# Rotary products of a second attention: from GpSimd and VectorE to VectorE alone

## The reference, cut to what matters

```python
# end of the mixture of experts: each token sums its four experts' rows
routed = sum over the 4 chosen slots of  weight * expert_ffn(x)
h = h + routed + shared
# second attention, 16 query heads, 4 key heads, head size 32
Q = layernorm(h) @ Wq ; K = layernorm(h) @ Wk ; V = layernorm(h) @ Wv
Q = Q * cos + rotate_half(Q) * sin
K = K * cos + rotate_half(K) * sin
A = softmax(causal(Q K^T / sqrt(32))) ; h = h + (A V) @ Wo
```

## Time and profile before

| | before |
|---|---|
| median of 3 runs | 1511.07 us (1508.02 to 1511.49) |
| the profiled execution's own time | 1511.43 us |
| its span, first to last instruction | 1509.5 us |
| PE busy | 1294.1 us (86%) |
| DVE busy | 896.4 us (59%) |
| ACT busy | 629.5 us (42%) |
| POOL busy | 308.6 us (20%) |
| mean granted TensorE clock | 0.922 of full |

### The profile page before, as it was taken

One profiled execution on the slowest core, in us unless ns is written; L12 is line 12 of the kernel. 1 busy time (PEld: TensorE's weight loads), 2 busy tenths in 40 slices (PEclk: granted clock), 3 DMA queues, 4 the chain that ended last, 5 costly groups with the idle time before them and its releaser, 6 DMA issues.

```text
span 1509.5 us, 30358 instructions
## 1 busy us (share of the span) xinstructions
PE 1294.1 (86%) x10660; PEld 829.6 (55%) x10674; DVE 896.4 (59%) x1865; ACT 629.5 (42%) x1066; POOL 308.6 (20%) x336
## 2 busy tenths in 40 slices
PE   6878899999999999986759999999972868768997
PEld 3446677777777877764424444444531656424443
DVE  5776455555565555668653555544332665578886
ACT  3445344444444444442314444444431333236664
POOL 2443000000000000000012233333267853010000
PEclk9997999999999999996779999999995869789999
DMA  5111343524435352422315767865268520000000
GB/s 181 68 66 43 100 178 138 200 105 174 142 127 204 135 185 109 156 85 89 124 70 178 257 227 257 303 242 170 98 125 133 85 43 3 2 1 8 21 21 32
DMA packets 44238, 184.26 MB, mean 122 GB/s; under 512 B 8688, under 2 KB 9200, under 8 KB 36368
## 3 DMA queue, kind: packets, MB, share of 16 engines
q0 software_dynamic: 21280, 95.41, 20.3%
q1 hardware_dynamic: 19440, 75.41, 14.3%
q10 hardware_dynamic: 3456, 12.58, 2.3%
HBM read 135.65 MB, written 47.73 MB: 121 GB/s over the span
## 4 chain that ended last, share of the span: by engine, by line
PE 55%; DVE 18%; issue 13%; POOL 7%; ACT 4%; DMA 2%; DVEq 1%; ACTq 0%; POOLq 0%; SPq 0%
PE ps L929 14%; PE ps L931 13%; PE ps L930 13%; POOL h L506 3%; PE ps L1036 3%; PE ps L1019 3%; PE ps L1255 2%; DVE ff L1976 2%; DVE amf L1983 1%; PE ps L1120 1%; PE ps L1052 1%; POOL rt_out L466 1%; PE ps L1348 1%; PE ps L1366 1%; POOL qraw L539 1%
## 5 line engine op out<-in xcount | busy, mean ns | idle before, releaser
L929 PE MATMUL ps<-nT_hi,wa_hi 128*128 128x368 f16 x448 | 147.9, 330 | 11.8 <-DVE wa_lo L1395 8.1
L930 PE MATMUL ps<-nT_lo,wa_hi 128*128 128x368 f16 x448 | 147.3, 329 | 0.0
L931 PE MATMUL ps<-nT_hi,wa_lo 128*128 128x368 f16 x448 | 147.0, 328 | 0.1
L496 POOL DMA_INDIRECT xg<-xrow,idx x61 | 61.4, 1007 | 276.7 <-PE ps L1120 121.5
L1559 DVE TENSOR_TENSOR a<-sq,E 92x368 f32<-92x368 f32 x64 | 31.7, 534 | 136.3 <-ACT sq L694 136.3
L1731 DVE SCALAR_TENSOR_TENSOR nrm<-ps,xg,nrm 128x256 f32<-128x256 f32 x61 | 29.5, 484 | 133.3 <-ACT nrm L737 112.1
L930 PE MATMUL ps<-wa_lo,nT_hi 128*92 128x128 f16 (+1 forms) x560 | 107.1, 235 | 0.0
L929 PE MATMUL ps<-wa_hi,nT_hi 128*92 128x128 f16 (+1 forms) x560 | 107.1, 235 | 0.0
L931 PE MATMUL ps<-wa_hi,nT_lo 128*92 128x128 f16 (+1 forms) x560 | 107.1, 235 | 0.0
L929 PE MATMUL ps<-wide,xT 128*128 x244 | 93.6, 383 | 12.9 <-issue 8.2
L491 POOL DMA_DIRECT2D wsp<-we_sp x16 | 8.6, 539 | 446.6 <-DVE we_sp L1395 446.6
(11 more groups left out here) (302 smaller groups left out, 3326.1 us busy)
## 6 DMA issues: line engine op xcount, KB each, us to landing
we_st<-in_we POOLq DMA_DIRECT2D x16, 1536.0 KB, 6.8
wsp<-we_sp POOLq DMA_DIRECT2D x16, 1536.0 KB, 5.4
wide<-wsp SPq DMA_DIRECT2D x16, 1536.0 KB
yslot<-yt POOLq DMA_DIRECT2D x61, 256.0 KB
wq_st<-in_ffq SPq DMA_DIRECT2D x24, 512.0 KB, 6.0
wq_st<-in_ffq ACTq DMA_DIRECT2D x24, 512.0 KB
wide<-in_wa SPq DMA_DIRECT2D x10, 1024.0 KB, 4.8
xt<-in_x SPq DMA_DIRECT2D x12, 512.0 KB, 3.5
```

The lines of the kernel that those rows point to most:

```text
L496: pool.indirect_dma_start(Q["xg"][:, g % 4, :].bitcast(U32), None, xrow, bass.IndirectOffsetOnAxis(ap=idx[:, g:g + 1], axis=0)).then_inc(x ...
L929: nc.tensor.matmul(dst, lhs[0], rhs[0], start=start, stop=False)
L930: nc.tensor.matmul(dst, lhs[0], rhs[1], start=False, stop=False)
L931: return nc.tensor.matmul(dst, lhs[1], rhs[0], start=False, stop=stop)
```

## The change

POOL no longer computes rotary products: `cosine` is gone. In `rotate(c, j)` DVE does the shuffle, the cosine product and the sine product, for every chunk and piece. POOL's list in that stretch keeps gathers, roots and memsets in another order: `shares(2, 1)` now stands ahead of `turned_root(0)`, `shares(2, 2)` ahead of `turned_root(1)`, `shares(3, 0)` behind `shares(2, 3)`, and `turned_root(2)` still behind `shares(3, 2)`. `rotated(c)` gets one count of a spare semaphore (`passed`) behind its wait.

```diff
--- before.py
+++ after.py
@@ -534,41 +534,25 @@
                 x = slice(GT * g, GT * g + GT)
                 root(rc_ask, 2 + g, rt_in[:, x], rt_out[:, x], rc_done)
 
-            def cosine(c, j):
-                pool.wait_ge(f_sh, 5 * c + j + 1)
-                nc.gpsimd.tensor_tensor(Fm["qraw"][:, j, :], Fm["qraw"][:, j, :], cosT[:], ALU.mult).then_inc(f_cos, 1)
-                if c and j < 4:
-                    nc.gpsimd.tensor_tensor(Fm["qs"][:, j, :], Fm["qs"][:, j, :], sinT[:], ALU.mult).then_inc(f_cos, 1)
-
             for j in range(TOPK):
                 shares(0, j)
                 shares(1, j)
             pool.wait_ge(m_y, VT)
             shares(2, 0)
+            shares(2, 1)
             turned_root(0)
             nc.gpsimd.memset(Fm["qp"][:, :, :, SL:], 0.0).then_inc(f_pad, 1)
+            shares(2, 2)
+            turned_root(1)
+            shares(2, 3)
             shares(3, 0)
-            turned_root(1)
-            cosine(0, 0)
-            shares(2, 1)
-            cosine(0, 1)
-            cosine(0, 2)
-            shares(2, 2)
-            cosine(0, 3)
-            cosine(0, 4)
-            shares(2, 3)
             pool.wait_ge(wa_lo, UNITS + 1)
             nc.gpsimd.memset(st_a[:], 0.0).then_inc(f_pad, 1)
             shares(3, 1)
-            for j in range(5):
-                cosine(1, j)
             shares(3, 2)
             turned_root(2)
             shares(3, 3)
             turned_root(3)
-            for c in range(2, CH):
-                for j in range(5):
-                    cosine(c, j)
             pipeline(pool, NT, [(0, lambda k, p, half: root(rf_ask, k, rt_in[:, p:p + 1], rt_out[:, p:p + 1], rf_done))])
             for n, x in enumerate((slice(0, EARLY), slice(EARLY, NT))):
                 root(rq_ask, n, rq_in[:, x], rq_out[:, x], rq_done)
@@ -1829,14 +1813,15 @@
                 dve.sem_inc(passed, 1)
                 V.stream_shuffle(Fm["qs"][:, j, :], Fm["qraw"][:, j, :],
                                  [(x + HD // 2) % HD for x in range(HD)]).then_inc(f_sh, 1)
-                if c == 0 or j == 4:
-                    dve.wait_ge(f_sh, 5 * c + j + 1)
-                    dve.sem_inc(passed, 1)
-                    V.tensor_tensor(Fm["qs"][:, j, :], Fm["qs"][:, j, :], sinT[:], ALU.mult).then_inc(f_cos, 1)
+                dve.wait_ge(f_sh, 5 * c + j + 1)
+                dve.sem_inc(passed, 1)
+                V.tensor_tensor(Fm["qraw"][:, j, :], Fm["qraw"][:, j, :], cosT[:], ALU.mult).then_inc(f_cos, 1)
+                V.tensor_tensor(Fm["qs"][:, j, :], Fm["qs"][:, j, :], sinT[:], ALU.mult).then_inc(f_cos, 1)
 
             def rotated(c):
 
                 dve.wait_ge(f_cos, 10 * c + 10)
+                dve.sem_inc(passed, 1)
                 if c:
                     dve.wait_ge(f_sc, c)
                 else:
```

## The result

The changed kernel took 1515.76 us (median of 6, 1514.63 to 1516.86), the kernel before 1510.45 us (median of 6, 1508.02 to 1511.49): ratio 1.0037, 95% interval 1.0024 to 1.0050. It is slower, by 5.3 us between the medians and 0.37% by the ratio. The profiled execution took 1516.86 us, with a span of 1515.1 us, 5.6 us more than before.

What follows compares the result with a forecast made beforehand. The second attention's start was taken to hang on `turned_root(0)` in POOL's list, each chunk being one chain. 5.7 - 2.65 - 1.9 - 0.1 + 1.85 + 1.5 = +4.4 on 1511.43 gave 1515.8 us, range 1510.5 to 1520.

Steps and rivals of the forecast that it cites:

- The root: Second attention's start: three gathers at 1.85 us ahead of `turned_root(0)`, uncovered, delay the first norm; +5.7 us.
- The landing wait: First gather of `shares(2, 1)` waits for slot 0 of the same tile to land: 0 to 1 us, 0.15 taken.
- Price of a product: Rotations on DVE: products start 0.46 us apart, so one rotation occupies DVE for 1.63 us.
- The rival of no overlap: Each DVE product occupies its full 0.54 us; chunks 1 to 3 cost 2.2 us more, 1518.0 us; chance 0.03.
- Stretching by gathers: POOL's gathers lengthen DVE's products in chunks 0 and 1: +4.7 us, 1520.5 us; chance 0.09.
- Chunks 1 to 3: DVE's rotations and weights up to `kr` replace the wait for POOL: -0.1, +1.85 and +1.5 us.
- Chunk 0: Before the first scores: PE becomes the limit, so only 2.66 of the 5.3 us `kr` waited come back; -2.65 us.
- Clock: `scores(0)` on PE: with the pause before it gone, it should run like `scores(2)`, 5.10 for 7.00 us; -1.9 us.
- The zero for the other three: Other three runs of scores may each gain or lose 1 to 2 us; their sum was taken as zero.
- The forecast's side of the 0.3% bound: Whether the time exceeds 1515.6 us, 0.3% slower: slower 0.51, same 0.43, faster 0.06.

Runs made afterwards that it cites:

- second pair of profiles: Kernel before and changed kernel each profiled again, unchanged: one run each, 1509.48 us and 1513.46 us.
- a division: Changed kernel with the old POOL order; in chunks 1 to 3 POOL does both products of pieces 0 to 2, DVE the others: 1500.57 us, ratio 0.9933.
- two versions with a short and a long pause: Changed kernel with chunk 0's `qp` addition repeated, two extra additions or three, to delay the first scores: 1518.40 us and 1523.87 us.

## Why the prediction was right, and where its terms were not

*The root.* Right in mechanism and place, +5.7 forecast, +6.1 in both pairs of profiles. The landing wait was 0.6 us and not 0.15. Putting the gathers back took 6.8 us off.

*Price of a product.* Right: pairs 0.46 apart, all 40 between 0.53 and 0.54 us long. The rival of no overlap fell. The Trainium skill (VectorE: DVE Perf Modes, section The DRAIN you can't avoid) adds to the rule that the prediction took from it that a next operation that is not held starts earlier; the 0.46 us agree with this exception, which the prediction left out. *Stretching by gathers* fell too: DVE's products ran beside gathers from 1173 to 1181 us unstretched. It is POOL's arithmetic that stretches, not its gathers.

*Chunks 1 to 3.* -0.1, +1.85 and +1.5 forecast; -0.1, +1.9 and +1.5 measured from rotation to `kr`. In chunk 2 0.4 us more came from PE, ahead of the second rotation. In the second pair of profiles this part was 0.25 us shorter after the change, and it goes with the clock, which rose 0.6 us (before) and 1.4 us (after) behind the first rotation in the first pair, 1.4 and 0.8 in the second.

*Chunk 0: mis-sized.* "Only 2.66 of the 5.3 us" came back; it was 4.3 and, in the second pair of profiles, 4.0. The limit was right, `qp` ended ahead of PE, but PE itself was 1.6 and 0.9 us earlier: its value projection had pauses before (ACT took its result 13.1 and 13.0 us behind the first rotation) and had none after (10.9 us both times). The value projection itself took 4.2 and 4.0 us before and 2.8 both times after; the clock is not the reason, since it was up throughout in all four. The old order with the products on DVE (3.0 us) and root 0 late with them on POOL (2.9 us) each lose most of the pauses in it as well. The profile puts these pauses down to issue, and what sets them stays open.

*Clock: right in sign for the first scores, mis-sized, and not by the cause given.* -1.9 forecast from the third scores of before; -3.2 and -2.3 measured. The prediction put the low clock down to PE's pause. The runs show the clock falling 20.5 us behind its rise with the pause and without it; the change helped because it brought the scores from 20.4 and 20.0 us behind the rise to 16.0 both times, by the pause that closed and by PE's shorter projections. So this term was in part luck. The third scores of before, from which it was taken, met the fall 2.3 us after their start, a chance value: they took 6.4 and 3.8 us in two executions of the changed kernel. The zero for the other three was +2.4 in the first pair, -0.9 in the second.

So the sum, +4.4, met +5.3 with chunk 0 and its scores 2.9 us too dear in the sum, and the landing wait, the later scores and the stretches behind them too cheap by as much and a little more. The root and chunks 1 to 3 are a sound hit; that the total came within 1 us is luck, as errors of about 3 and 4 us went against each other. The forecast's side of the 0.3% bound was barely more than even; the measured interval, 0.24% to 0.50%, includes that bound.

## What to carry to other kernels

Look for the instruction for which every other engine stands idle, and count each gather ahead of it at full price: three gathers moved past one small root cost more than 32 products moved between engines gave back. When work leaves the slower engine, divide it by the time that each engine has free in each stage; all to the fast one gave nothing in chunk 1 and cost 1.9 and 1.5 us in chunks 2 and 3, while a division gained 10 us. Once an ordering change is down to 2 us, the TensorE clock in short stages can decide more than the order does, so profile the same kernel twice before explaining such a difference. And before a slow burst of matmuls is put down to the pause ahead of it, look where the granted clock rose and fell: two versions with a short and a long pause seemed to prove that cause, and their clock didn't bear it out.

## What the runs showed of the hardware

The 128 small matmuls of the scores took 3.8 us at 2.4 GHz and 7.0 us at 1.2 GHz. In chunk 0 the clock rose during the first projections and, in both profiles of the kernel before and of the changed one, stayed up for 20.48 us, with pauses of PE of 2.66 and 3.13 us ahead of the scores or with none. It fell in the changed kernel although PE had been busy for all of the 20.48 us, and the next projections ran at 0.50 of the clock from 1192.5 to 1195.9 us. Behind pauses of 0.84 and 0.90 us, two executions of this kernel gave 6.4 and 3.8 us for the third scores.

A VectorE product with two SBUF inputs takes 0.53 to 0.58 us beside gathers of GpSimd, and 0.55 to 1.99 us beside a product of GpSimd. A gather took 5.5 us from its start to its landing in the kernel before, and 10.7 us in one case where a 1 MB load had been issued 1 us behind it.
